# Four-layer cross attention: weight folds in two row groups of TensorE, three homes for their results, keys, values and wo requested elsewhere

## The chip, the cores and the metric

One core of a Trainium2 chip runs the whole program. The metric is the device time of one execution in microseconds, the median over runs.

## What is computed

`x` (4 x 1024 x 512) passes through four cross attentions on one context `ctx` (4 x 64 x 1024): grouped, masked, grouped, masked.

```
grouped: xn = rmsnorm(x) * norm_w; q = xn @ wq (16 heads of 32); k, v = ctx @ wk, ctx @ wv (4 heads of 32)
         x = x + softmax(q k^T / sqrt(32)) v @ wo
masked:  q = x @ Wq (16 heads of 64); k, v = ctx @ Wk, ctx @ Wv (16 heads of 64)
         logits = q k^T / 8 + bias of two pairs of key columns from the token masks
         x = x + softmax(logits) v @ Wo + bo
```

All is float32. TensorE multiplies most matrices in three products of a high part (rounded to the format fp32r) and the rest: hi*hi + hi*lo + lo*hi.

## The kernel before

**Folds.** In the masked layers Wq is multiplied into the keys and Wo into the values ahead of time: per layer, 8 key folds and 8 value folds, each for one pair of heads, 32 in all (`MASKED`). `m_made(n)` (24 matmuls of 256 columns) makes 128 rows (two heads of 64) of k^T or v^T for all four batches in bank `OB`. ScalarE (`kv_hi`) and VectorE (`kv_lo`) spread it as high and low part into `bd`, a 128 x 512 block diagonal tile, zero where a row's head isn't the column's. `folding(n)` multiplies it with the weight block `fhl`: 4 banks of 3 matmuls, each 512 columns wide over all 128 rows. `taken_out(n)` copies two banks by ScalarE and two by VectorE into a home in SBUF (`staged`, two homes in turn), and SyncE's queue stores them to DRAM in 4 transfers of 256 KB (`f_store`), beside the loads of 512 KB (`w_load`) and 256 KB (`f_load`) for each fold.

**Order.** It is written out by hand. PE runs `m_made(n)`, then `folding(n-1)`, for n = 0 to 23 (`EARLY`), with six small products for the grouped layers between (`g_made`); then the query product of the first token block (`q_bound`), and then `grouped_first`: 8 times scores of the grouped layer, `m_made`, `folding`. ScalarE's program for step n is `kv_hi(n)`, `w_hi(n+4)`, `taken_out(n-1)`, `f_hi(n+1)`; VectorE's `kv_lo(n)`, `w_lo(n+4)`, `taken_out(n-1)`, `f_lo(n+1)`. `folding(n)` waits until `taken_out(n-1)` has freed its banks. At n = 12 to 15 ScalarE also rounds the four pieces of the grouped layer's wq (`ws_hi`). At n = 20 it waits for `bias_b` twice counted, then rounds and squares two pieces of x (`x_hi`) into `xqhl` and `xsq`.

**GpSimd.** It scales wq by the norm weights (`ws_scale`), makes the bias of the second layer in the scratch tile `xsq`, waits for the four `ws_hi` with `ws_lo`, then makes the bias of the fourth layer in the same scratch, and counts `bias_b` (lines 1183 to 1226). That is why `x_hi`, which writes `xsq`, waits for it (line 748).

**After the folds** 8 rounds over batches and layer pairs (`body`) run on each of two token blocks; they load the folds back in 16 pieces of 256 KB through `ring`, the last 8 from `sFN` (`ring_load`, line 344). ScalarE rounds each and GpSimd takes the rest (`part_lo`, line 1260). The first round needs wo of the grouped layer in `wraw`, which SyncE requests after the last store (line 284).

Of the kernel before, what the change touches and what calls it, by code (L numbers as in the profile page):

```python
# [14 lines left out]
P = 128  # L15
BATCH = 4
# [26 lines left out]
def bass_cross_attention_stack(nc, xT, ctxT, wkvM, wkvG, wqG, woG, wqM, woM, normw, bo, masks, idx, xs):  # L43
# [12 lines left out]
    with ctx:  # L56
# [8 lines left out]
        sFN = nc.dram_tensor("s_fn", (PAIRS, BATCH, KC, P, D), F32, kind="Internal").ap()  # L65
        sKG = nc.dram_tensor("s_kg", (PAIRS, BATCH, 2, P, KEYS), F32, kind="Internal").ap()
# [47 lines left out]
        names = ("ctx_in cx_hi cx_lo w_hi w_lo made taken g_hi kv_hi f_hi f_lo folded ev_a ev_d "  # L114
# [8 lines left out]
        f_st = [sem(f"s_f_st{i}") for i in range(2)]  # L123
        wg_in = [sem(f"s_wg_in{i}") for i in range(2)]
# [14 lines left out]
        bd = [foldM[:, :, i, 0:HALF] for i in range(2)]  # L139
# [20 lines left out]
        def staged(n, o):  # L160

            if n % 2 == 0:
                return ring[:, o, :] if n < 8 else X[0][:, o, :]
            if n < EARLY:
                return prob[0][:, 2 + o // 2, (o % 2) * BLK:(o % 2 + 1) * BLK]
            return wraw[:, o, :]

        def pair(n, part, r):

            rows = slice(64 * r, 64 * r + 64)  # L170
            return bd[n % 2][rows, part, :].rearrange("p (b h k) -> p b h k", b=BATCH, h=2)[:, :, r, :]

        def t_bank(ph, t):

            return MX if ph in (0, 3) and t % 2 else TB

# [12 lines left out]
        def _(sp):  # L189
            sp.dma_start(cx, ctxT).then_inc(S["ctx_in"], 16)  # L190
            for n in range(2):
                sp.dma_start(wG[:, n], wkvG[0, n]).then_inc(wg_in[n], 16)
# [12 lines left out]
            def f_store(n):  # L205
                lp, t = n // (2 * KC), n % KC
                for o in range(4):
                    if o < 2:
                        sp.wait_ge(S["ev_a"], 2 * n + o + 1)
                    else:  # L210
                        sp.wait_ge(S["ev_d"], 2 * n + o - 1)
                    if n // KC % 2 == 0:
                        sp.dma_start(sFM[lp, t, o].rearrange("p b n -> p (b n)"), staged(n, o)).then_inc(f_st[n % 2], 16)
                    else:
                        sp.dma_start(sFN[lp, o, t], staged(n, o)).then_inc(f_st[n % 2], 16)

            def g_store(lp, i):
                sp.wait_ge(S["taken"], g_step(lp, i) + 1)
                if i == 0:
                    for b in range(BATCH):  # L220
                        sp.dma_start(sKG[lp, b].rearrange("s p k -> p s k"),
                                     stK[lp][:, :, b * KEYS:(b + 1) * KEYS].bitcast(F32)).then_inc(g_st[lp], 16)
                else:
                    sp.dma_start(sVG[lp, 2 * (i - 1):2 * i].rearrange("b k n -> (b k) n"),
                                 stV[lp][:, i - 1]).then_inc(g_st[lp], 16)

            def kg_load(it):
                for r in range(4):
                    sp.dma_start(kG4[32 * r:32 * r + 32, :, :, KEYS * r:KEYS * (r + 1)].bitcast(F32),
                                 sKG.rearrange("l b s (j d) k -> (l b) d s j k", d=HD_G)[it]).then_inc(S["ld_kg"], 16)  # L230
# [17 lines left out]
            for n in range(4, MASKED + 9):  # L248
                if n < MASKED:
                    w_load(n)  # L250
                if n == 5:
                    for i in range(GROUP):
                        g_store(0, i)
                    for i in range(2):
                        sp.dma_start(wG[:, i], wkvG[1, i]).then_inc(wg_in[i], 16)
# [4 lines left out]
                if n >= 9:  # L260
                    f_store(n - 9)
                if 4 <= n - 3 < MASKED:
# [3 lines left out]
                if n == 19:  # L266
                    sp.wait_ge(S["zero"], 3)
                    for i in range(PAIRS):
                        sp.wait_ge(g_st[i], (BATCH + 2) * 16)
                    kg_load(0)  # L270
                if n == 21:
                    vg_load(0)
                if n == 20:
                    sp.wait_ge(f_st[0], 4 * 64)
# [7 lines left out]
            sp.wait_ge(f_st[1], 16 * 64)  # L282
            sp.wait_ge(S["ws_lo"], DC)
            sp.dma_start(wraw[:, :, :], woG[0]).then_inc(S["ld_w"], 16)
            sp.wait_ge(f_st[0], 16 * 64)
            sp.dma_start(X[0][:, :, :], xT[0, 0]).then_inc(S["ld_x0"], 16)

            def body(it, lp, first, last):
# [43 lines left out]
                if not first:  # L332
# [10 lines left out]
                for t in range(KC):  # L343
                    ring_load(t % 4, sFN[lp, b, t], ("fb_lo", 12 * it + t + 1))
# [10 lines left out]
        def _(pe):  # L355
# [8 lines left out]
            pe.wait_ge(S["ctx_in"], 16)  # L364

            def g_made(lp, i):
# [3 lines left out]
                if i < 2:  # L370
                    pe.wait_ge(wg_in[i], 16 * (lp + 1))
                for c in range(CC):
                    if i == 0:
# [20 lines left out]
            def folding(n):  # L394
                if n == 0:
                    pe.wait_ge(S["zero"], 3)
                pe.wait_ge(S["taken"], m_step(n) + 1)
                pe.wait_ge(S["f_lo"], n + 1)
                w, kv = fhl[n % 2], bd[n % 2]
                for o in range(4):  # L400
                    cut = slice(o * P, (o + 1) * P)
                    if n > 0 and o < 2:
                        pe.wait_ge(S["ev_a"], 2 * n + o - 1)
                    elif n > 0:
                        pe.wait_ge(S["ev_d"], 2 * n + o - 3)
                    if n // KC % 2 == 0:
                        last = three(FB[o][:, :], w[:, 0, cut], w[:, 1, cut], kv[:, 0, :], kv[:, 1, :], True, True)
                    else:
# [972 lines left out]
```

## Time and profile before

| | us |
|---|---|
| median of 3 runs (1568.18 to 1569.41) | 1569.0 |
| the profiled execution | 1568.2 |
| its span, first to last instruction | 1566.4 |
| PE busy in it | 1549.7 |
| folds 0 to 23 and what makes them, on PE | 15.9 to 158.0 |
| folds 24 to 31, with grouped scores | 170.1 to 221.2 |

A timeline row gives start and length in us, engine, line, operation, written tile <- read tiles, and a count. Matmuls are pipelined, so lengths of neighbours overlap: the pace is the distance between starts. `three` (lines 359 to 361) issues nearly all matmuls, so rows are told apart by their tiles: `OB<-xhl,foldN` is `m_made` in the early part, `<-foldM,pT` and `<-pT,foldM` are folds.

### The profile page before, as it was taken

Reading aid. Unit: us, or ns where it says so; the run is one execution under the profiler, and the core shown is the slowest. Engines: PE = TensorE matmul, PEld = TensorE weight load, DVE = VectorE, ACT = ScalarE, POOL = GpSimd, SP = SyncE. Lnnn points to the kernel's source line nnn. Section 1 sums busy time; section 2 is a strip of 40 time slices with the busy share of each in tenths; the row PEclk is TensorE's granted clock in tenths of the full one; section 3 lists DMA queues with packets and bytes.
Section 4 is the critical chain, followed back from the end, with each engine's and each line's share of the span. In section 5 each row is a group of like instructions: output and inputs, shape, how many; then the busy total and the mean of one; then the engine's idle time right before and its main releaser. Section 6 shows DMA issues by size and latency. Waiting matters only on the chain.

```text
span 1566.4 us, 22435 instructions
## 1 busy us (share of the span) xinstructions
PE 1549.7 (99%) x8032; PEld 1260.3 (80%) x8032; DVE 1025.5 (65%) x1697; ACT 770.5 (49%) x1349; POOL 882.8 (56%) x809
## 2 busy tenths in 40 slices
PE   8999999999999999999999999999999999999998
PEld 7999887788778877788778877887778877887787
DVE  6777657765566657665776556665766577655664
ACT  4566666425643465335642564346533564256431
POOL 0523357546864676467754685467645775468431
PEclk9999999999999999999999999999999999999999
DMA  9999563122321331122312232133112231222101
GB/s 345 317 331 375 200 222 99 53 70 94 115 61 31 129 115 47 34 90 76 114 51 69 94 115 61 31 131 113 47 35 94 75 111 52 66 95 88 54 1 54
DMA packets 110237, 170.58 MB, mean 109 GB/s; under 512 B 27568, under 2 KB 60848, under 8 KB 103984
## 3 DMA queue, kind: packets, MB, share of 16 engines
q1 hardware_dynamic: 107232, 151.85, 29.7%
q10 hardware_dynamic: 2736, 16.78, 2.6%
q8 instruction: 65, 1.06, 0.3%
q0 software_dynamic: 160, 0.53, 0.1%
q14 instruction: 44, 0.36, 0.1%
HBM read 117.48 MB, written 51.65 MB: 108 GB/s over the span
## 4 chain that ended last, share of the span: by engine, by line
PE 94%; POOL 3%; DMA 1%; DVE 1%; ACT 0%; issue 0%; SPq 0%
PE OB L359 17%; PE OB L361 17%; PE OB L360 17%; PE SB L359 10%; PE SB L361 9%; PE SB L360 9%; PE TB L480 5%; PE MX L516 4%; PE MX L480 2%; POOL xhl L1268 1%; POOL prob L1233 1%; PE SB L459 1%; POOL prob L1239 1%; DMA prob<-in_wkvM_dram 1%; PE TB L361 0%; PE TB L359 0%
## 5 line engine op out<-in xcount | busy, mean ns | idle before, releaser
L1239 POOL TENSOR_TENSOR prob<-prob,small 128x512 f32<-128x512 f32 x256 | 277.8, 1088 | 288.7 <-DVE small L1041 288.7
L1233 POOL TENSOR_TENSOR prob<-prob,small 128x512 f32<-128x512 f32 x128 | 136.3, 1065 | 147.8 <-DVE small L1016 147.7
L1022 DVE SCALAR_TENSOR_TENSOR prob<-SB,aux 128x512 f32<-128x512 f32 x128 | 88.1, 688 | 198.9 <-PE SB L361 198.9
L359 PE MATMUL SB<-foldM,xhl 128*128 128x512 f32 x512 | 203.0, 396 | 4.5 <-POOL xhl L1268 2.7
L359 PE MATMUL OB<-pT,foldN 128*128 128x512 f32 x512 | 205.0, 400 | 0.0
L360 PE MATMUL OB<-pT,foldN 128*128 128x512 f32 x512 | 199.8, 390 | 0.0
L361 PE MATMUL OB<-pT,foldN 128*128 128x512 f32 x512 | 199.8, 390 | 0.0
L361 PE MATMUL SB<-foldM,xhl 128*128 128x512 f32 x512 | 199.6, 390 | 0.0
L360 PE MATMUL SB<-foldM,xhl 128*128 128x512 f32 x512 | 199.4, 389 | 0.0
L762 ACT ACTIVATE prob<-prob 128x512 f32<-128x512 f32 x128 | 80.5, 629 | 173.6 <-DVE prob L1028 172.2
L1016 DVE TENSOR_REDUCE small<-prob 128x8 f32<-128x512 f32 x128 | 87.4, 683 | 109.8 <-ACT prob L771 109.8
L480 PEld LDWEIGHTS TB<-ident,prob 128*128 128x128 f32 x768 | 90.3, 140 | 52.9 <-issue 32.5
L771 ACT ACTIVATE prob<-SB 128x512 f32<-128x512 f32 x128 | 76.5, 597 | 106.3 <-PE SB L361 102.6
L1247 POOL TENSOR_TENSOR xqhl<-ring,xqhl 128x512 fp32r<-128x512 f32 x64 | 82.9, 1306 | 69.4 <-ACT xqhl L702 69.4
L359 PEld LDWEIGHTS SB<-foldM,xhl 128*128 128x128 f32 x512 | 96.1, 188 | 31.9 <-POOL xhl L1268 9.8
L480 PE MATMUL TB<-ident,prob 128*128 128x128 f32 x768 | 117.7, 276 | 0.0
L1028 DVE TENSOR_TENSOR prob<-prob,small 128x512 f32<-128x512 f32 x128 | 111.1, 868 | 4.5
L361 PEld LDWEIGHTS OB<-pT,foldN 128*128 128x128 f32 x512 | 96.1, 188 | 20.9
L361 PEld LDWEIGHTS SB<-foldM,xhl 128*128 128x128 f32 x512 | 96.1, 188 | 20.7
L360 PEld LDWEIGHTS SB<-foldM,xhl 128*128 128x128 f32 x512 | 96.2, 188 | 19.2
L359 PEld LDWEIGHTS OB<-pT,foldN 128*128 128x128 f32 x512 | 96.4, 188 | 18.2 <-DVE pT L919 0.3
L360 PEld LDWEIGHTS OB<-pT,foldN 128*128 128x128 f32 x512 | 96.5, 188 | 17.1
(157 smaller groups left out, 3927.3 us busy)
## 6 DMA issues: line engine op xcount, KB each, us to landing
prob<-in_wkvM_dram SPq DMA_DIRECT2D x32, 512.0 KB, 6.4
ring<-s_fm SPq DMA_DIRECT2D x64, 256.0 KB, 5.1
ring<-s_fn SPq DMA_DIRECT2D x64, 256.0 KB, 2.7
out_dram<-x ACTq DMA_DIRECT2D x15, 1024.0 KB, 3.9
s_fm<-prob SPq DMA_DIRECT2D x32, 256.0 KB, 5.0
wraw<-in_wqG_dram SPq DMA_DIRECT2D x8, 1024.0 KB, 8.5
s_fn<-x SPq DMA_DIRECT2D x32, 256.0 KB, 4.9
ring<-in_xT_dram SPq DMA_DIRECT2D x32, 256.0 KB, 3.3
```

What stands on the lines that cost most here:

```text
L359: pe.matmul(out, a_hi, b_hi, start=start, stop=False)
L360: pe.matmul(out, a_hi, b_lo, start=False, stop=False)
L361: return pe.matmul(out, a_lo, b_hi, start=False, stop=stop)
L480: last = pe.transpose(out[:, tt * P:(tt + 1) * P], pr[:, tt, t * P:(t + 1) * P], ident[:, :])
L762: act.activation(own, own, ACT.Exp).then_inc(S["exped"], 1)
L771: act.activation(prob[ph][:, u % 4, (u // 4) * HALF:(u // 4 + 1) * HALF], SB[u % 2][:, :], ACT.Copy).then_inc(S["copied"], 1)
L1016: dve.reduce_max(hmax[u % 2], own, AX_X).then_inc(S["maxed"], 1)
L1022: dve.scalar_tensor_tensor(out=own, in0=bank, scalar=M_SCALE, in1=row, op0=ALU.mult, op1=ALU.add).then_inc(S["biased"], 1)
L1028: dve.tensor_tensor(own, own, hmax[u % 2].unsqueeze(2).broadcast_to([P, HH, KEYS]), ALU.subtract).then_inc(S["evac"], 1)
L1233: pool.tensor_tensor(own, own, hmax[u % 2].unsqueeze(2).broadcast_to([P, HH, KEYS]), ALU.subtract).then_inc(S["evac"], 1)
L1239: pool.tensor_tensor(own, own, rsum[u % 2].unsqueeze(2).broadcast_to([P, HH, KEYS]), ALU.mult).then_inc(S["normed"], 1)
L1247: pool.tensor_tensor(xqhl[:, 1, c % 2, :], ring[:, c, :], xqhl[:, 0, c % 2, :].bitcast(F32), ALU.subtract).then_inc(S["x_lo"], 1)
```

## The change

The folds work per head. `kv` holds the rows as they are (128 x 256, no zeros). Head 0 lies in rows 0 to 63 and head 1 in rows 64 to 127 of both operands; each matmul takes 64 rows, and the two heads' alternate and write different banks. A key fold has 24 matmuls of 64 rows x 256 columns, a value fold 12 of 64 rows x 512 columns. ScalarE takes out head 0's banks, VectorE head 1's. There are six homes and stores of 512 KB; folds 8 to 23 use three in turn. `sFN` and `sKG` have other layouts: a piece of `sFN` comes back in two transfers of 64 partitions, and the grouped keys are stored in one transfer with rows of 1 KB. The first loads are split in halves. ScalarE requests the first grouped keys at its steps 12 to 15; the grouped values and wo are requested by SyncE after the store of fold 29. wq goes to `wraw` later (SyncE's n = 16 where it was 11), and ScalarE rounds it at its steps 17 to 20, where it was 12 to 15. VectorE's first four memsets are gone. GpSimd's program is as it was.

```diff
-        bd = [foldM[:, :, i, 0:HALF] for i in range(2)]
+        kv = [foldM[:, :, i, 0:BATCH * KEYS] for i in range(2)]
...
+        STAGES = (ring, lower, upper, X[0], wraw, X[1])
+        HOME = ((0, 2, 4, 0, 2, 4, 0, 2) + (3, 1, 2) * 5 + (3,)
+                + (4, 3, 4, 3, 4, 3, 5, 3))
...
@@ sync @@
+                    sp.dma_start(dst, staged(n)[:, 2 * i:2 * i + 2, :]).then_inc(f_st[HOME[n]], 16)
...
+                if n - 9 == MASKED - 3:
+                    sp.wait_ge(f_st[4], 32 * stores(4))
+                    sp.wait_ge(S["ws_lo"], DC)
+                    sp.dma_start(wraw[:, :, :], woG[0]).then_inc(S["ld_w"], 16)
...
+                    vg_load(0)
...
-                if n == 11:
+                if n == 16:
+                    sp.wait_ge(f_st[4], 32 * 2)
                     sp.dma_start(wraw[:, :, :], wqG[0]).then_inc(S["ld_w"], 16)
...
                 for t in range(KC):
-                    ring_load(t % 4, sFN[lp, b, t], ("fb_lo", 12 * it + t + 1))
+                    sp.wait_ge(S["fb_lo"], 12 * it + t + 1)
+                    for r in range(2):
+                        sp.dma_start(ring[64 * r:64 * r + 64, t % 4, :],
+                                     sFN[lp, t, b // 2, r, 64 * (b % 2):64 * (b % 2) + 64, :]).then_inc(ld_ring[t % 4], 16)
@@ tensor, folding(n) @@
+                w, x = fhl[n % 2], kv[n % 2]
+                parts = ((0, 0), (0, 1), (1, 0))
+                for i in range(2):
+                    if n > 0:
+                        pe.wait_ge(S["ev_a"], 2 * n + i - 1)
+                        pe.wait_ge(S["ev_d"], 2 * n + i - 1)
+                    for a in range(2 if n // KC % 2 == 0 else 1):
+                        for m, (p, q) in enumerate(parts):
+                            for r in range(2):
+                                rows = slice(64 * r, 64 * r + 64)
+                                if n // KC % 2 == 0:
+                                    cut = slice((2 * i + a) * P, (2 * i + a + 1) * P)
+                                    last = pe.matmul(FB[2 * i + r][:, 256 * a:256 * a + 256], w[rows, p, cut], x[rows, q, :],
+                                                     start=(m == 0), stop=(m == 2))
+                                else:
+                                    last = pe.matmul(FB[2 * i + r][:, :], x[rows, p, i * P:(i + 1) * P], w[rows, q, :],
+                                                     start=(m == 0), stop=(m == 2))
                     last.then_inc(S["folded"], 1)
@@ scalar @@
-                for r in range(2):
-                    src = OB[m_step(n) % 2][64 * r:64 * r + 64, 0:BATCH * KEYS].rearrange("p (b k) -> p b k", b=BATCH)
-                    last = act.activation(pair(n, 0, r), src, ACT.Copy)
+                act.activation(kv[n % 2][:, 0, :], OB[m_step(n) % 2][:, 0:BATCH * KEYS], ACT.Copy).then_inc(S["kv_hi"], 1)
...
-                if 12 <= n < 12 + DC:
-                    ws_hi(0, n - 12)
+                if 17 <= n < 17 + DC:
+                    ws_hi(0, n - 17)
+                if 12 <= n < 16:
...
+                    act.dma_start(*kg_part(0, n - 12)).then_inc(S["ld_kg"], 16)
                 if n == 20:
                     for i in range(PAIRS):
-                        act.wait_ge(g_st[i], (BATCH + 2) * 16)
+                        act.wait_ge(g_st[i], 3 * 16)
                     act.wait_ge(S["bias_b"], PAIRS)
                     x_hi(0, 0, 0, True)
                     x_hi(0, 0, 1, True)
@@ vector, kv_lo(n): one operation of 128 x 256 for two of 64 x 256; taken_out as ScalarE's @@
```

## Rows read from the trace of the kernel before

**Rows 1.** The page, part 1: span and PE's busy time, share, count.
```profile
span 1566.4 us, 22435 instructions
PE 1549.7 (99%) x8032; PEld 1260.3 (80%) x8032; DVE 1025.5 (65%) x1697; ACT 770.5 (49%) x1349; POOL 882.8 (56%) x809
```
**Rows 2.** Windows: stretch, length, busy us by engine (count), granted clock, DMA share, GB/s.
```profile
100.00:120.00 20.00, 20.00 (x131) 18.31 (x130) 16.68 (x22) 12.79 (x24) 10.53 (x17) 1.00 1.01 334
120.00:140.00 20.00, 20.00 (x131) 18.25 (x130) 15.48 (x23) 12.72 (x23) 6.93 (x11) 1.00 1.04 401
...
178.00:197.00 19.00, 19.00 (x128) 17.52 (x127) 17.70 (x30) 13.80 (x25) 6.91 (x7) 1.00 0.75 263
```
**Rows 3.** PE's timeline: two folds' first matmuls, one make's, two folds' among scores.
```profile
21.75 0.40 PE L359 MATMUL OB<-foldM,pT 128*128 128x512 f32 x1
...
24.50 0.28 PE L359 MATMUL OB<-xhl,foldN 128*128 128x256 f32 x1
...
27.37 0.40 PE L359 MATMUL OB<-foldM,pT 128*128 128x512 f32 x1
...
177.65 0.40 PE L359 MATMUL OB<-pT,foldM 128*128 128x512 f32 x1
...
183.99 0.40 PE L359 MATMUL OB<-pT,foldM 128*128 128x512 f32 x1
```
**Rows 4.** PE's timeline: eight loads with one-column matmuls, then column tiles of 64.
```profile
169.25 0.95 PE L459 MATMUL SB<-small,sqsum 128*128 128x1 f32 x8
170.06 0.37 PE L359 MATMUL SB<-kG,foldM 128*128 128x256 f32 x1
...
239.55 0.39 PE L361 MATMUL OB<-foldN,wqo 128*128 128x512 f32 x1
239.87 1.08 PE L516 MATMUL MX<-pF,vG 128*64 128x512 f32 x4
240.88 0.33 PE L480 MATMUL TB<-ident,prob 128*128 128x128 f32 x1
```
**Rows 5.** The weight loads' timeline (PEld) at those column tiles.
```profile
239.87 0.20 PEld L516 LDWEIGHTS MX<-pF,vG 128*64 128x64 f32 x4 [0.36 <-issue]
```
**Rows 6.** ScalarE's timeline in its step n = 20.
```profile
135.76 0.77 ACT L685 ACTIVATE foldM<-OB 64x256 fp32r<-64x256 f32 x2 [0.38 <-PE OB L361]
136.55 1.06 ACT L669 ACTIVATE foldN<-prob 128x1024 fp32r<-128x1024 f32 x1
...
139.67 0.63 ACT L702 ACTIVATE xqhl<-ring 128x512 fp32r<-128x512 f32 x1
```
**Rows 7.** Groups by form, 60 to 150 us: busy us, mean ns, idle before.
```profile
L919 DVE TENSOR_TENSOR foldN<-prob,foldN 128x1024 fp32r<-128x1024 f32 x17 | 21.9, 1288 | 3.7 <-ACT foldN L669 3.6
...
L919 DVE TENSOR_TENSOR foldM<-OB,foldM 64x256 fp32r<-64x256 f32 x32 | 13.5, 422 | 11.7 <-ACT foldM L685 11.5
...
L962 DVE COPY prob<-TB 128x512 f32<-128x512 f32 x8 | 5.5, 692 | 1.1 <-DMA s_fn<-prob 0.8
```
**Rows 8.** GpSimd's timeline: the last ws_lo, and the store after the second bias.
```profile
111.90 1.29 POOL L1165 TENSOR_TENSOR wqo<-wraw,wqo 128x512 fp32r<-128x512 f32 x1 [4.49 <-ACT wqo L719]
...
127.11 0.61 POOL L1226 DMA_DIRECT2D s_aux<-aux  x1 [0.31 <-POOL aux L1224]
```
**Rows 9.** PE's timeline: the same 16 matmuls after idling and in midstream.
```profile
7.04 5.24 PE L374 MATMUL OB<-prob,x 128*128 128x256 f32 x16 [7.04 <-DMA x<-in_wkvG_dram]
...
35.74 3.61 PE L374 MATMUL OB<-prob,x 128*128 128x256 f32 x16
```
**Rows 10.** SyncE's timeline: the requests for the grouped keys.
```profile
92.71 1.94 SPq L229 DMA_DIRECT2D kG<-s_kg  x4
```
**Rows 11.** PE's timeline after wo has come.
```profile
231.37 1.08 PE L516 MATMUL MX<-pF,vG 128*64 128x512 f32 x4 [0.93 <-ACT pF L779]
```
**Rows 12.** GpSimd's timeline: the first round's first piece of sFN split.
```profile
278.31 1.28 POOL L1262 TENSOR_TENSOR foldN<-ring,foldN 128x512 fp32r<-128x512 f32 x1
```
**Rows 13.** PE's timeline: the product that reads that piece.
```profile
302.97 0.47 PE L359 MATMUL OB<-pT,foldN 128*128 128x512 f32 x1
```

More of the change, by code:

```diff
@@ L112, in bass_cross_attention_stack @@
         FB = [OB[2], OB[3], TB, MX]
-        names = ("ctx_in cx_hi cx_lo w_hi w_lo made taken g_hi kv_hi f_hi f_lo folded ev_a ev_d "
+        names = ("cx_hi cx_lo w_hi w_lo made taken g_hi kv_hi f_hi f_lo folded ev_a ev_d "
                  "ld_w ws_scaled ws_hi ws_lo c_in c_norm "
@@ L254, in _ @@
                     for i in range(2):
-                        sp.dma_start(wG[:, i], wkvG[1, i]).then_inc(wg_in[i], 16)
+                        for h in range(2):
+                            sp.dma_start(wG[:, i, 4 * h:4 * h + 4], wkvG[1, i, :, 4 * h:4 * h + 4]).then_inc(wg_in[2 * i + h], 16)
                     f_load(2)
@@ L331, in body @@
                 sp.dma_start(aux[:, :], sAux[lp]).then_inc(S["ld_aux"], 16)
-                if not first:
+                if first:
+                    sp.wait_ge(f_st[5], 32 * stores(5))
+                else:
                     sp.wait_ge(S["stored1"], 16 * it)
@@ L361, in three @@
                 return pe.matmul(out, a_lo, b_hi, start=False, stop=stop)
[L364 removed]
+            pe.wait_ge(cx_in[0], 16)
             def g_made(lp, i):
@@ L511, in mixing @@
                     pe.wait_ge(S["ld_vg"], 64 * (it + 1))
+                    if first and ph == 1:
+                        pe.wait_ge(S["ev_d"], 2 * MASKED)
                 if j > 0 or ph == 2:
@@ L785, in part_hi @@
             def part_hi(it, i, first):
-                act.wait_ge(ld_ring[i % 4], 16 * (6 * it + (2 if i < 4 and not first else 3 + i // 4)))
+                if i < 4:
+                    act.wait_ge(ld_ring[i % 4], 16 * (8 * it + (3 if first else 2)))
+                else:
+                    act.wait_ge(ld_ring[i % 4], 16 * (8 * it + 2 * (1 + i // 4)))
                 act.activation(fold_part(i, 0), ring[:, i % 4, :], ACT.Copy).then_inc(S["fold_hi"], 1)
@@ L923, in _ @@
             dve.memset(small[:, 12:16], -0.5).then_inc(S["idented"], 1)
-            for i in range(2):
-                for part in range(2):
-                    last = dve.memset(bd[i][:, part, :].bitcast(F32), 0.0)
-            last.then_inc(S["zero"], 1)
             dve.memset(kG[:, :, :].bitcast(F32), 0.0).then_inc(S["zero"], 1)
@@ L949, in kv_lo @@
                 dve.wait_ge(S["kv_hi"], n + 1)
-                for r in range(2):
-                    src = OB[m_step(n) % 2][64 * r:64 * r + 64, 0:BATCH * KEYS].rearrange("p (b k) -> p b k", b=BATCH)
-                    last = lo_part(pair(n, 1, r), src, pair(n, 0, r))
-                last.then_inc(S["taken"], 1)
+                lo_part(kv[n % 2][:, 1, :], OB[m_step(n) % 2][:, 0:BATCH * KEYS], kv[n % 2][:, 0, :]).then_inc(S["taken"], 1)
             def taken_out(n):
-                for o in range(2, 4):
-                    dve.wait_ge(S["folded"], 4 * n + o + 1)
-                    if n >= 2 and o == 2:
-                        dve.wait_ge(f_st[n % 2], 64 * (n // 2))
-                    if n == EARLY + 1 and o == 2:
+                for i in range(2):
+                    dve.wait_ge(S["folded"], 2 * n + i + 1)
+                    if uses(n) and i == 0:
+                        dve.wait_ge(f_st[HOME[n]], 32 * uses(n))
+                    if n == EARLY and i == 0:
                         dve.wait_ge(S["ws_lo"], DC)
-                    dve.tensor_copy(staged(n, o), FB[o][:, :]).then_inc(S["ev_d"], 1)
+                    to, out = own(n, i, 1)
+                    dve.tensor_copy(to, out).then_inc(S["ev_d"], 1)
             for h in range(2):
```

137 lines of the change are left out of this document (65 added, 72 removed).

## The prediction

> **What bounds the kernel now.** The page comes first: PE is busy for 1549.7 of 1566.4 us [rows 1], so whatever shortens the run has to take time off PE or fill one of its few gaps. The windows over the fold stretch come next: the granted clock is 1.00, PE is full, and at the same time the DMA engines' share is 1.01 to 1.04 [rows 2]. Two things are near their limit there, PE and memory traffic, and the reader is to see that traffic was 334 GB/s in one window and 401 in the next, with PE's matmul count alike. PE's timeline then prices a step: a fold runs from 21.75 to 24.50, 2.75 us for 12 matmuls of 512 columns (0.229 each); the make up to 27.37 takes 2.87 for 24 of 256 (0.120 each). A step is 5.62. Among the scores it is 183.99 - 177.65 = 6.34 [rows 3]. The rest of the run, 8 rounds at full PE, is touched by the change only through smaller transfers.
>
> **The fold on PE.** The same products are done without the zeros. If both row groups stream at once, a key fold is 12 pairs of 256 columns, 12 x 0.120 = 1.44 us, a value fold 6 pairs of 512, 6 x 0.229 = 1.37. No row shows row groups. The nearest are the column groups of `mixing`: four passes of 512 columns, started at 239.87, are over at 240.88 [rows 4]. One after another they would take at least four times 0.427 (the pace of 512 columns in two passes; two of 0.213 by the 0.229 less its overhead), 1.7 us, so the two groups do overlap; and their four weight loads lie within 0.20 us [rows 5]. I take full overlap. The bounds are 1.37 and, without overlap, 24 x 0.120 = 2.87.
>
> Between full and tiled use PE pays. The matmul before `mixing` starts at 239.55 and has streamed by 239.78; the tiled one starts at 239.87, 0.09 later. On both ways the first weight load, elsewhere hidden, lies bare: eight loads with a one-column matmul each take 170.06 - 169.25 = 0.81, about 0.10 each [rows 4]. So 0.4 us per fold, bounds 0.2 and 0.5. A key fold comes to 1.84 (saves 0.91), a value fold to 1.77 (saves 0.98). Folds 0 to 23 are 16 and 8 of them: 14.6 + 7.8 = 22.4 us. PE's step is then 4.71.
>
> One rule speaks against this. The Trainium skill, "TensorE: Matmul & The Clock Gate", section on LDWEIGHTS, has a load priced by its columns and not by its rows, so that a load of 64 rows costs as much as one of 128. Its page "TensorEngine Tiling (Array Packing)", key properties, lets different tiles load in parallel, and says that a change of mode drains the engine. The 0.10 of the one-column row agrees with the first, the 0.20 us for four loads with the second, the 0.09 with the third. If the loads of two row groups came one after another, a key fold would gain nothing: that is rival C.
>
> **The other engines in a step.** ScalarE's step is 0.4 for keys (one operation for two of 0.38), 1.06, two copies of 0.5, 0.5 for the weights: 3.1 us, 3.7 with `ws_hi` [rows 6]. Each request for grouped keys is 1.94 / 4 = 0.49 [rows 10]; on ScalarE it makes steps 12 to 15 3.6 us, or 4.1 if one takes twice as long: still under 4.71, so nothing. VectorE loses one of two 0.42 operations and keeps 1.29, two of 0.69 and the weights' part, under 4 us [rows 7]. Copies with strided targets are like the strided 64 x 256 ones of now, at no more per element.
>
> **DMA.** A step moves 512 + 256 + 4 x 256 KB = 1.835 MB. In 4.71 us that is 390 GB/s; one window shows 401, another 334 at a share of 1.01 [rows 2]. I take 401 as possible, since it was had when SyncE had requests in arrears, and charge 2 us for folds 0 to 19 (0 to 12.5: at 334 a step is 5.49 and 16 steps give up 0.78 each). Three homes take away waits of the copies for a store; none of those reached PE before, so 0 by itself. The Trainium skill, "DMA: Bandwidth & Descriptors", specifications, gives a core about 358 GB/s of HBM; by it a step would be at least 5.1 us. The row of 401 contradicts it here.
>
> **The new wait.** This is the term that I weigh most. `x_hi` at ScalarE's n = 20 waits for the second bias, because it writes the scratch in which GpSimd makes it. GpSimd starts that bias only after the last `ws_lo`, and so after the last `ws_hi`. From the start of that `ws_lo`, 111.90, to the count just before the store, 127.11 - 0.31 = 126.80, it takes 14.9 us [rows 8]. Before, ScalarE came to `x_hi` at 139.67 [rows 6], 12.9 us after that. Now the last `ws_hi` is itself at n = 20, directly ahead of the wait. GpSimd's program is unchanged, so ScalarE stands for 14.9 us. What is queued behind: `x_hi` and squares (four starts 0.52 apart, 2.1), `kv_hi(21)`, `w_hi(25)`, `taken_out(20)`. From the end of `m_made(20)`: `ws_hi` ends at 3.8, the bias at 18.7, x at 20.8, `kv_hi(21)` at 21.2, `w_hi(25)` at 22.2; VectorE's `w_lo(25)` ends at 23.5, its first copy of fold 20 at 24.2, and `folding(21)` can start at 24.3. PE meanwhile has done two folds and two makes, 2 x 4.71 = 9.4. It idles 14.9 us (bounds 12.5, if GpSimd runs faster beside idle neighbours, and 15.5). Then it starts slow: the same 16 matmuls took 5.24 us after 7.04 us of idling and 3.61 in midstream, 1.6 more [rows 9] (0 to 3). After that every wait for `taken_out` is met again.
>
> **Folds among scores.** 8 value folds save 0.98 on PE, step 5.36. VectorE was busy 17.70 of 19 us, 5.9 per step, in the first ones [rows 2]; less 0.42 that is 5.5, and it becomes the bound for four of them: 4 x 0.84 + 4 x 0.98 = 7.3 us (5 to 7.9).
>
> **wo and grouped values.** wo lands two steps earlier. PE's gap of 0.93 behind it [rows 11] goes: 0.9 (0 to 0.9). wq later: SyncE asks for it with the store of fold 7, some nine steps (42 us) before ScalarE's step 17, and scaling takes GpSimd a few operations like those in rows 8: nothing.
>
> **Halved transfers of sFN.** 64 more requests on SyncE, which is idle most of a round. The first piece is ready on GpSimd at 278.31 + 1.28 = 279.6 and is multiplied at 302.97 [rows 12, 13]: 23 us of cover; 0, and if it were gone 0.5 us per piece.
>
> **First loads, memsets.** Making starts when the second masked weight block has landed behind all earlier bytes, and these are the same: 0 (-1 to +1).
>
> **Sum.** -22.4 + 14.9 + 1.6 + 2.0 - 7.3 - 0.9 = -12.1. The profiled execution took 1568.2, which gives 1556.1; the median of before is 0.8 above it, so **1557 us**.
>
> **Rivals.**
> A. The second bias is not waited for at length (it ends earlier than I read, or something frees ScalarE). Then 16.5 fall away: 1568.2 - 28.6 + 0.8 = 1540. For it: GpSimd is idle most of this stretch. Against it: the order of GpSimd's program, fixed.
> B. Memory traffic bounds folds 4 to 19 at the 334 GB/s of the weaker window: 12.5 for the 2.0, less what the stand lets it catch up, sum -1.6: 1567. For it: share above 1 at 334. Against it: 401.
> C. The weight loads of the two row groups come one after another. A key fold is 24 x 0.101 + 0.4 = 2.82 (+0.07), value folds keep their gain (12 loads in 1.21). 16 x 0.07 - 7.8, PE idles 24.3 - 11.4 = 12.9, + 1.6 - 7.3 - 0.9 = -0.4: 1569. For it: 0.10 per load. Against it: four loads in 0.20.
> D, on the other side: row groups do not overlap at all. Key folds 24 x 0.120 + 0.4 = 3.28 (+0.53), value folds 12 x 0.229 + 0.4 = 3.15 (+0.40); 11.7 in the first 24, 12.0 + 1.6 for the wait, 3.2 among scores, -0.9: +27.6, **1597**. It turns from gain to loss once a pair takes over about 0.19 us in place of 0.12. For it: no row has row groups, and none has tiles in fp32r. Against it: `mixing`.
>
> **How the numbers follow.** Forecast 0.60 (its own range 1550 to 1564, from the bounds of the terms), A 0.07, B 0.14, C 0.08, D 0.11. What can't be told from no change is 0.2%, 3 us. Faster: the forecast, A and most of B (0.09), 0.76; within: the rest of B and C, 0.13; slower: D, 0.11. The range 1541 to 1572 leaves out D and half of A.
>
> **What would show it.** Row pairs started a few ns apart and 1.4 us of streaming per fold (against C, D); a step of 4.7 on PE before fold 20; one gap of about 15 us on PE near 125 us with ScalarE waiting for GpSimd's aux, and slow matmuls behind it; then steps of 5.4 to 5.5 among the scores; no gap before the first `mixing`; rounds 2 to 8 as long as before. I am wrong if that gap is absent, if a pair takes the time of two, or if steps before it are over 5 us with SyncE never waiting.

## The result, and the profile after

The changed kernel takes **1558.7 us** (median of 4 runs, 1558.5 to 1560.3), the kernel before 1569.2 beside it (1568.2 to 1569.6). The ratio is 0.9938 [0.9924, 0.9951]; the forecast was 1557. The profiled execution took 1558.5 us with a span of 1556.7; before they were 1568.2 and 1566.4 [rows 1], so the spans differ by 9.7. The first `mixing` starts 9.70 earlier than before (221.67 for 231.37) and one of the last round 9.60 (1471.42 for 1481.02): all of it lies ahead of 240 us, and rounds 2 to 8 are as long as before.

The fold on TensorE (PE in the rows), the first key fold behind the last of the grouped products (start and length in us, engine, line, operation, written tile <- read tiles, count). It answers to [rows 3].

```profile
54.62 0.98 PE L431 MATMUL OB<-foldM,pT 64*128 64x256 f32 x12
55.91 0.28 PE L431 MATMUL TB<-foldM,pT 64*128 64x256 f32 x1
55.92 0.28 PE L431 MATMUL MX<-foldM,pT 64*128 64x256 f32 x1
56.03 0.28 PE L431 MATMUL TB<-foldM,pT 64*128 64x256 f32 x1
56.04 0.28 PE L431 MATMUL MX<-foldM,pT 64*128 64x256 f32 x1
56.24 0.39 PE L379 MATMUL OB<-xhl,foldN 128*128 128x256 f32 x1
```

Two matmuls of different row groups start 10 ns apart, a pair each 0.12 us, and the fold is over after 56.24 - 54.62 = 1.62 us, where it took 2.75. The make behind it is longer, 3.06 for 2.87. A value fold takes 1.59 and its step 4.64.

Then the long gap. First TensorE, then ScalarE, GpSimd and VectorE of the changed kernel around it; the bracket is the idle time before the row and who ended it:

```profile
129.79 0.28 PE L381 MATMUL OB<-xhl,foldN 128*128 128x256 f32 x1
144.87 1.65 PE L431 MATMUL OB<-foldM,pT 64*128 64x256 f32 x12 [14.80 <-DVE x L993]
147.72 0.58 PE L379 MATMUL OB<-xhl,foldN 128*128 128x256 f32 x1
155.59 0.97 PE L431 MATMUL OB<-foldM,pT 64*128 64x256 f32 x12 [1.75 <-DVE prob L993]
```

```profile
124.42 0.60 ACT L723 ACTIVATE prob<-OB 128x512 f32<-128x512 f32 x1 [1.29 <-DMA s_fm<-prob]
125.91 0.63 ACT L747 ACTIVATE wqo<-wraw 128x512 fp32r<-128x512 f32 x1
138.54 0.63 ACT L730 ACTIVATE xqhl<-ring 128x512 fp32r<-128x512 f32 x1 [11.99 <-POOL aux L1255]
140.63 0.36 ACT L711 ACTIVATE foldM<-OB 128x256 fp32r<-128x256 f32 x1
140.89 1.04 ACT L699 ACTIVATE foldN<-prob 128x1024 fp32r<-128x1024 f32 x1
```

```profile
126.62 1.28 POOL L1196 TENSOR_TENSOR wqo<-wraw,wqo 128x512 fp32r<-128x512 f32 x1 [3.33 <-ACT wqo L747]
127.89 3.33 POOL L1223 TENSOR_SCALAR xsq<-xsq,sqsum 128x64 f32<-128x64 f32 x8
137.11 1.26 POOL L1255 TENSOR_TENSOR aux<-aux,spare 128x512 f32<-128x512 f32 x1
```

```profile
141.02 0.42 DVE L956 TENSOR_TENSOR foldM<-OB,foldM 128x256 fp32r<-128x256 f32 x1 [14.28 <-ACT foldM L711]
141.97 2.15 DVE L956 TENSOR_TENSOR foldN<-prob,foldN 128x1024 fp32r<-128x1024 f32 x1 [0.52 <-ACT foldN L699]
144.04 0.68 DVE L993 COPY x<-OB 128x512 f32<-128x512 f32 x1
```

Read from the back: fold 21 waits for VectorE's copy, VectorE stood 14.28 us for ScalarE's `kv_hi`, ScalarE stood 11.99 us in front of `x_hi` for GpSimd's `aux`, and GpSimd began that bias only after the last `ws_lo`. PE's row says "<-DVE", but the cause is three engines back. The 1.75 before fold 23 (the last PE row) is another matter, taken up with the first experiment.

The windows of the changed kernel (busy time of each engine, then granted clock, DMA share, GB/s), against [rows 2]:

```profile
60.00:80.00 20.00, 20.00 (x178) 17.60 (x175) 14.62 (x22) 12.65 (x23) 0.80 (x1) 1.00 1.02 391
80.00:100.00 20.00, 20.00 (x159) 17.33 (x158) 17.18 (x23) 12.17 (x22) 19.18 (x30) 1.00 1.05 405
100.00:120.00 20.00, 19.77 (x191) 18.26 (x189) 13.93 (x20) 11.16 (x20) 4.14 (x4) 1.00 1.05 402
134.00:144.00 10.00, 0.00 (x0) 0.00 (x0) 2.46 (x2) 5.46 (x11) 8.38 (x10) 0.50 0.25 96
144.00:158.00 14.00, 11.39 (x99) 10.63 (x100) 10.07 (x16) 6.38 (x11) 0.00 (x0) 0.76 0.93 296
```

DMA kept 391 to 405 GB/s for 60 us. TensorE's granted clock fell to 0.50, the lower of its two levels, within the gap and stayed there until 150.8: fold 21 took 2.85 us and the make behind it 4.42.

Two folds among the scores of the changed kernel, 5.36 us apart where it was 6.34:

```profile
176.69 0.96 PE L434 MATMUL OB<-pT,foldM 64*128 64x512 f32 x6
182.05 0.73 PE L434 MATMUL OB<-pT,foldM 64*128 64x512 f32 x4
```

**Where the time went**, by the same landmarks in both traces (after less before, running total): first make 17.66 for 15.92, +1.7. Fold 20 starts at 125.32 for 141.18, -15.9, so the twenty steps from fold 0 to fold 19, with the makes beside them, brought 17.6. Query product at 157.20 for 158.08, -0.9: the stretch with the gap costs 15.0 net. Second query product at 212.29 for 221.15, -8.9: scores brought 8.0, of which the eight folds 7.8. The gap of 0.93 before the first `mixing` [rows 11] is gone, -9.7, the difference of the spans.

### The profile page after: what moved, and what is told of

The parts are those of the page before. It is cut to its first block, busy times and chain, and to the rows that moved or that the text cites. A ratio compares the mean times of both kernels' runs of the same rounds, so it can differ in the third digit from the quotient of the medians.

```text
span 1556.7 us, 22870 instructions
## 1 busy us (share of the span) xinstructions
PE 1522.4 (98%) x8224; PEld 1233.7 (79%) x8224; DVE 1004.1 (64%) x1661; ACT 750.1 (48%) x1317; POOL 881.2 (57%) x809
## 4 chain that ended last, share of the span: by engine, by line
PE 90%; POOL 4%; DVE 2%; DMA 1%; ACT 1%; issue 1%; SPq 1%; ACTq 0%; DVEq 0%; POOLq 0%
PE OB L379 16%; PE OB L381 15%; PE OB L380 15%; PE SB L379 10%; PE SB L381 9%; PE SB L380 9%; PE TB L508 5%; PE MX L546 4%; POOL xhl L1299 2%; PE MX L508 2%; POOL prob L1264 1%; PE SB L487 1%; DMA s_fm<-prob 1%; PE OB L434 1%; PE OB L431 1%
```

## Experiments

All are variants of the changed kernel but one; each was timed against the kernel before. Kernels that have undivided first loads count lines from `three` on three to five lower, that with wo last one lower.

### Where the long gap comes from

**Weights rounded early.** ScalarE rounds wq at its steps 12 to 15 again.

```diff
-                if 17 <= n < 17 + DC:
-                    ws_hi(0, n - 17)
+                if 12 <= n < 12 + DC:
+                    ws_hi(0, n - 12)
```

> The changed kernel, with ScalarE rounding wq at its steps 12 to 15 as before and not 17 to 20; all else as changed. My theory: the 14.8 us for which PE idles at 130 us, the slow clock after it (2.6 us over the fold at 144.87 and the make at 147.72) and the 1.75 us gap before fold 23 all come from x_hi waiting for the second bias. GpSimd will have done its first bias at 100.8, four ws_lo by 106 and the second bias by about 119, before ScalarE comes to x_hi at 126. Then 19 us go, less 1 to 3 us for folds 20 to 23, which memory traffic (400 to 410 GB/s from 70 to 134 us) will hold up: 1541 to 1543 us, no gap over 3 us before 160 us. Rival 1 (the stand only shows a backlog of DMA that has to be drained anyway, landings being 10 us and more late): PE idles 8 to 12 us somewhere before 158 us, 1552 us or more. Rival 2 (the stand is x_hi's wait for its pieces of x or for the grouped stores): nothing changes, 1558.

Measured 1544.95 us, 0.9848 [0.9835, 0.9862]. The gap of 14.8 is gone and `x_hi` does not wait. But 13.7 us came back and not the whole of gap and slow clock, and the time is 2 us above what was expected. There is a new, small gap; VectorE and GpSimd of this kernel at that place, and TensorE with every gap of 0.3 us and more from there to the query product:

```profile
102.74 5.40 DVE L956 TENSOR_TENSOR foldN<-prob,foldN 128x1024 fp32r<-128x1024 f32 x1 [0.53 <-ACT foldN L699]
108.07 0.68 DVE L993 COPY prob<-OB 128x512 f32<-128x512 f32 x1
```

```profile
102.01 5.02 POOL L1196 TENSOR_TENSOR wqo<-wraw,wqo 128x512 fp32r<-128x512 f32 x4
107.02 5.70 POOL L1223 TENSOR_SCALAR xsq<-xsq,sqsum 128x64 f32<-128x64 f32 x8
```

```profile
108.89 0.86 PE L431 MATMUL OB<-foldM,pT 64*128 64x256 f32 x10 [2.92 <-DVE prob L993]
141.89 0.98 PE L431 MATMUL OB<-foldM,pT 64*128 64x256 f32 x12 [1.75 <-DVE prob L993]
```

VectorE's `w_lo`, elsewhere 1.23 us, takes 5.40 and ends at 108.14: 1.1 us after 107.03, when GpSimd's four `ws_lo` in a row were over. PE idles 2.92 and then runs 3.4 us at 0.5.

The second row shows that the 1.75 before fold 23 has nothing to do with the long gap: it stands here too. Folds 22 and 23 follow each other with no make between, so fold 23 waits for VectorE's copies of fold 22, and VectorE is held up by `kv_lo` and `w_lo` before them. From the start of fold 22 to that of fold 23 it is 3.44 us here, with folds of 1.62 and a gap of 1.75, and again 3.44 with folds of 1.96 (heads in turn, gap 1.40) and of 3.06 (one row group, gap 0.31). In the kernel before, with folds of 2.75, fold 23 follows after 2.82 without a gap. It is the faster fold that lays this wait bare.

**Bias first.** GpSimd makes the second bias ahead of the four `ws_lo`; the weights stay late.

```diff
-                    for c in range(DC):
-                        ws_lo(0, c)
...
+            for c in range(DC):
+                ws_lo(0, c)
```

> The changed kernel with one move on GpSimd alone: the second bias is made ahead of the four ws_lo. ScalarE's program is as changed. My theory: the bias is then done at about 114 us, x_hi waits for nothing, and the time is that of the experiment that rounds wq early, within 1 us: 1541 to 1543. Rival 1 (DMA backlog): 1552 or more. Rival 2 (it was rounding wq at steps 17 to 20 that made ScalarE late, not the wait): 1555 to 1558.

1546.92 us, 0.9861 [0.9848, 0.9875]. The order on GpSimd alone removes the long gap too. It is 4 us above what was expected: gaps of 1.41 and 2.00 stand in its place, beside the 1.75 before fold 23; at the first, `f_lo` took 3.38 us beside two `ws_lo` in a row.

**The late weights in the kernel before.** wq requested at SyncE's step 16 and rounded at 17 to 20, all else as before.

```diff
-                if n == 11:
+                if n == 16:
                     sp.dma_start(wraw[:, :, :], wqG[0]).then_inc(S["ld_w"], 16)
...
-                if 12 <= n < 12 + DC:
-                    ws_hi(0, n - 12)
+                if 17 <= n < 17 + DC:
+                    ws_hi(0, n - 17)
```

> The kernel before with one part of the change alone: wq requested at SyncE's n = 16 and rounded at ScalarE's steps 17 to 20. My theory: the stand comes from this move alone, whatever the folds cost. From the end of the make of step 20: wq rounded at 4.2, bias 12.2 later (as measured after the change) at 16.4, x at 18.5, keys, weights and VectorE's copy until fold 21 can start at 22.4; PE is busy for two of its steps, 11.2, so it idles 11 us, and then runs slow for 2 to 3 us: 1569.2 + 13 to 14 = 1583. Rival (the stand needs the faster folds, the longer steps of before give GpSimd the time): 1569 to 1571.

1582.35 us, 1.0086 [1.0069, 1.0102], 13.9 more than the kernel before beside it (1568.46), as expected. PE idles 10.34 before fold 21. The same row appears on its ScalarE, with nothing else of the change present:

```profile
152.75 0.63 ACT L702 ACTIVATE xqhl<-ring 128x512 fp32r<-128x512 f32 x1 [12.50 <-POOL aux L1224]
```

So the late weights cost 13.9 in the old kernel and 13.7 in the new one, and the rest of the change gives about 24.

### What the row groups give

**One row group.** Both heads read rows 0 to 63, in the same matmul count and shapes; the products of head 1's rows are left out.

```diff
-                                rows = slice(64 * r, 64 * r + 64)
+                                rows = slice(0, 64)
```

> The changed kernel with both heads' fold matmuls reading rows 0 to 63 of both operands; head 1's rows are left out of the folds. Instructions, banks, waits and order are the same, but neighbours are in one row group and cannot overlap. My theory: row groups alone give the gain. A key fold then takes 24 x 0.120 + 0.15 = 3.0 and a value fold 12 x 0.229 + 0.15 = 2.9 instead of 1.6 each; 32 x 1.35 = 43, less 3 at the idle time before fold 21: +40, 1599 us. Rival (a matmul of 64 rows streams faster by itself): folds of 1.6 to 2.2 us and under 1575. The trial with the heads in turn, which cost 3.3 us only, is explained by my theory only if TensorE drew the other group's matmuls ahead; here it can't, so a fold must show 2.9 to 3.1.

1597.72 us, 1.0187 [1.0173, 1.0201], as expected. TensorE of this kernel at a fold's end:

```profile
26.30 0.28 PE L431 MATMUL TB<-foldM,pT 64*128 64x256 f32 x1
26.42 0.28 PE L431 MATMUL MX<-foldM,pT 64*128 64x256 f32 x1
26.54 0.28 PE L431 MATMUL TB<-foldM,pT 64*128 64x256 f32 x1
26.66 0.28 PE L431 MATMUL MX<-foldM,pT 64*128 64x256 f32 x1
26.87 0.38 PE L379 MATMUL OB<-xhl,foldN 128*128 128x256 f32 x1
```

The same rows follow each other at 0.12 where they fell in pairs. Key folds take 3.06, value folds 2.94. That the two groups overlap is worth 39 us, and without it the change would lose: rival D's mechanism, at about its price.

**Heads in turn.** The loop over heads goes outside, so that a bank pair is done for head 0 and then for head 1.

```diff
-                    for a in range(2 if n // KC % 2 == 0 else 1):
-                        for m, (p, q) in enumerate(parts):
-                            for r in range(2):
+                    for r in range(2):
+                        for a in range(2 if n // KC % 2 == 0 else 1):
+                            for m, (p, q) in enumerate(parts):
```

> The changed kernel with the two heads' matmuls of a fold no longer alternating: all of head 0's of a half fold, then all of head 1's. Same instructions, other order. My theory: the gain of the folds is the overlap of neighbouring matmuls in different row groups. Without it a key fold takes 24 x 0.120 and a value fold 12 x 0.229 plus the change of mode, about 1.5 us more each; the idle time before fold 21 shrinks by 3 us, since PE is busy longer beside it. 32 x 1.5 - 3 - 1 = +44: 1602 us. Rival 1 (memory traffic bounds the early steps anyway, PE has room): only the 8 folds among scores lose, +12: 1571. Rival 2 (TensorE finds the overlap by itself, pulling the other group's matmuls ahead): 1559.

1561.99 us, 0.9959 [0.9944, 0.9974]: missed by 40. TensorE of this kernel, in the same key fold:

```profile
62.56 0.28 PE L431 MATMUL OB<-foldM,pT 64*128 64x256 f32 x1
62.56 0.28 PE L431 MATMUL TB<-foldM,pT 64*128 64x256 f32 x1
62.92 0.28 PE L431 MATMUL MX<-foldM,pT 64*128 64x256 f32 x1
62.92 0.28 PE L431 MATMUL TB<-foldM,pT 64*128 64x256 f32 x1
63.15 0.52 PE L431 MATMUL MX<-foldM,pT 64*128 64x256 f32 x3
```

In each pair above one matmul stands three instructions behind the other in the program; the first of TB started at 62.45, ahead of the last two of OB (62.56 and 62.68), which come before it. Matmuls of a free row group are started ahead of those of a busy one. Only the ends of a fold stay alone, and a key fold takes 1.96 for 1.62, a value fold 1.59 as before. Alternating in the code is worth 3.3 us, not 40.

### The parts priced at nothing

**Two homes.** Folds 8 to 23 use two homes in turn.

```diff
-        HOME = ((0, 2, 4, 0, 2, 4, 0, 2) + (3, 1, 2) * 5 + (3,)
+        HOME = ((0, 2, 4, 0, 2, 4, 0, 2) + (1, 3) * 8
```

> The changed kernel with folds 8 to 23 in two homes in turn (lower, X[0]) instead of three. Stores land 7 to 13 us after their request between 100 and 130 us, with steps of 4.64 us. My theory: two homes give a store 9.3 us less the copies, so copies wait and PE with them from about fold 12 on: PE loses 0.5 to 2 us a step until SyncE and DMA are in step, 3 to 10 us before the stand at 130 us, none after it: 1562 to 1569. Rival (DMA throughput, not homes, sets the pace; the third home only moves the wait from the copies to the loads): 1558 to 1560, within 0.1%.

1564.03 us, 0.997 [0.9959, 0.9982], 5.4 more than the change, in the range expected. ScalarE of this kernel:

```profile
102.65 0.60 ACT L723 ACTIVATE prob<-OB 128x512 f32<-128x512 f32 x1 [3.42 <-DMA s_fn<-prob]
109.15 0.60 ACT L723 ACTIVATE x<-OB 128x512 f32<-128x512 f32 x1 [3.68 <-DMA s_fn<-x]
```

The copies wait for the store of the fold before last, and PE idles 1.06, 1.33 and 1.80 behind them, with 3.4 us at 0.5 after the last.

**Whole first loads.** Context and weight blocks each come in one transfer again.

```diff
-            for h in range(2):
-                sp.dma_start(cx[:, 4 * h:4 * h + 4], ctxT[:, 4 * h:4 * h + 4]).then_inc(cx_in[h], 16)
-                sp.dma_start(wG[:, 0, 4 * h:4 * h + 4], wkvG[0, 0, :, 4 * h:4 * h + 4]).then_inc(wg_in[h], 16)
-            for h in range(2):
-                sp.dma_start(wG[:, 1, 4 * h:4 * h + 4], wkvG[0, 1, :, 4 * h:4 * h + 4]).then_inc(wg_in[2 + h], 16)
+            sp.dma_start(cx, ctxT).then_inc(cx_in[0], 16)
+            for i in range(2):
+                sp.dma_start(wG[:, i], wkvG[0, i]).then_inc(wg_in[2 * i], 16)
```

> The changed kernel with the first loads whole as before (context 1 MB, each grouped weight 512 KB) instead of in halves. My theory: the halves, with rows of 2 and 4 KB, moved 258 GB/s in the stretch 2 to 6 us where whole ones moved 355, so the second masked weight block landed at 13.1 and not at 11.4, and the first make began at 17.66 and not at 15.92. With whole loads the first make starts at 15.9 to 16.1 and the time falls by 1.7 us to 1557. Rival (the three additional requests on SyncE, 0.45 us each, are what is late, not the bytes): the same 1.3 to 1.7 us, but with DMA at 336 or more in both kernels' stretch 2 to 6 us. Rival 2 (it is the product order or VectorE's missing memsets): first make still at 17.6, 1558.6.

1557.12 us (1556.9 to 1557.3), 0.9924 [0.9911, 0.9938], 1.5 less than the change. The stretch from 4 to 6 us of its windows, and of the changed kernel's:

```profile
4.00:6.00 2.00, 0.00 (x0) 0.00 (x0) 0.15 (x1) 0.43 (x1) 0.00 (x0) 1.00 0.97 399
```

```profile
4.00:6.00 2.00, 0.00 (x0) 0.00 (x0) 0.19 (x2) 1.06 (x1) 0.00 (x0) 1.00 0.96 266
```

The share of busy DMA time is the same, but half loads move 266 GB/s where whole ones move 399. That holds in every trace of this document: 256 to 296 GB/s in these 2 us in the seven kernels with halves, 375 to 401 in the seven with whole loads. Halves are both smaller and in rows half as long, and no run separates the two. The first make starts at 16.92 for 17.66, and not at 15.92 as before. In this kernel the clock rose at 12.9 us, in the kernel before at 10.2; over the other kernels it lay between 9.6 and 13.1, so part of a start is chance. Over all traces the first make starts at 17.47 to 18.66 with halves and at 15.92 to 17.03 with whole loads, so the halves can account for all of the 1.7.

**wo and grouped values last.** Both requests move behind the last store.

```diff
-                if n - 9 == MASKED - 3:
-                    sp.wait_ge(f_st[4], 32 * stores(4))
-                    sp.wait_ge(S["ws_lo"], DC)
-                    sp.dma_start(wraw[:, :, :], woG[0]).then_inc(S["ld_w"], 16)
...
-                    vg_load(0)
```

> The changed kernel with wo and the grouped values requested after the last fold's store, as wo was before. My theory: PE's gap of 0.8 to 0.9 us at the first mixing comes back, and the four requests for the values in front of the token block add up to 2 us to what mixing waits for: 1559.5 to 1561.5. Rival (nothing on the path, since the second query product covers it): 1558.6.

1563.2 us, 0.9961 [0.9948, 0.9975], 4.5 more than the change and 2 more than expected at most. The profiled execution is the longest of the five, 1565.7. SyncE's queue, ScalarE and the first `mixing` of this kernel:

```profile
215.85 1.19 SPq L295 DMA_DIRECT2D wraw<-in_woG_dram  x1
217.13 3.78 SPq L252 DMA_DIRECT2D vG<-s_vg  x4
221.76 6.17 SPq L322 DMA_DIRECT2D ring<-s_fm  x4
```

```profile
225.05 0.63 ACT L746 ACTIVATE wqo<-wraw 128x512 fp32r<-128x512 f32 x1 [6.02 <-DMA wraw<-in_woG_dram]
227.25 1.23 PE L545 MATMUL MX<-pF,vG 128*64 128x512 f32 x4 [3.56 <-ACT pF L811]
```

What `mixing` waits for is wo: ScalarE stands 6.02 us until it has landed, 8 us after its request was through, and only then comes to the `pF` that `mixing` reads. In the kernel before ScalarE stood 3.39 at that place. The values' four requests come behind that of wo, so they can't delay the request; why wo takes longer to land than in the kernel before (4.7 us) is open. PE idles 3.56 and runs 3.4 us at 0.5. This trace also has a late first make (18.29 for 17.66) and 3.4 us of slow clock behind the gap before fold 23, so not all of the 4.5 need be wo's.

### A better version

**Early weights and whole first loads** (the first and the fourth edit together).

> The changed kernel with wq rounded at steps 12 to 15 and with whole first loads together. If the two gains are apart: 1558.7 - 17 - 1.7 = 1540. If memory traffic is the bound for folds 4 to 23 once the stand is gone, the 1.7 us of the start are kept, since bytes come sooner too; if PE then only waits longer for DMA, 1541.5, as with the first alone.

1543.73 us (1543.3 to 1545.6), 0.9841 [0.9827, 0.9854]. That is 2 us and more above both figures expected. The gap beside the four `ws_lo` remains, 2.40, and so does the 1.75 before fold 23.

**Weights spaced.** The same with `ws_hi` at steps 14 to 17, so that `ws_lo` don't run four in a row.

```diff
-                if 17 <= n < 17 + DC:
-                    ws_hi(0, n - 17)
+                if 14 <= n < 14 + DC:
+                    ws_hi(0, n - 14)
```

> The kernel with whole first loads and early rounding of wq (1543.7), with wq rounded at ScalarE's steps 14 to 17 instead of 12 to 15. In that one GpSimd was late with the first bias and then ran its four ws_lo in a row from 102.0 to 107.0; VectorE's w_lo, which began at 102.7, took 5.40 us instead of 1.2 to 1.3, PE idled 2.4 us and ran 3.4 us at the granted clock 0.5. My theory: VectorE's operation was held up by GpSimd's row of operations without a break. With the roundings later than the first bias, each ws_lo runs alone, no w_lo takes over 2.6 us there, the gap and the slow clock go: 3 to 4 us less, 1540. Second bias done at about 122, x_hi wanted at 125. Rival (the long w_lo comes from traffic into SBUF, 400 GB/s then, not from GpSimd): still one w_lo over 4 us and 1543 to 1544. Rival 2 (once PE is not held up, it meets the DMA backlog two folds later): 1542 to 1543.

1545.26 us, 0.9849 [0.9835, 0.9862], a miss. `w_lo` took 3.09 beside two `ws_lo`, and that gap shrank to 0.60. But the second bias was done at 125.65 only, `x_hi` waited 1.26 us, its own four operations take 2.1, and PE idled 3.46 at 128.74 and was slow for 6.8.

**Spaced, and x one step later** (the block of `n == 20` at 21).

```diff
-                if n == 20:
+                if n == 21:
```

> The kernel of e8 (whole first loads, weights rounded at n = 14 to 17) with ScalarE's block of x_hi moved from n = 20 to n = 21. There x_hi waited 1.26 us for a bias that was done at 125.65, and TensorE idled 3.46 us and then ran at half clock for 6.8 us. My theory: one step (4.6 us) later the bias is done before ScalarE comes, the gap of 3.46 and its slow stretch go (3.46 + about half of the folds' work in 6.8, less what VectorE makes up: 4 to 5 us), the 0.60 gap near 104 stays: 1545.3 - 4 to 5 = 1540 to 1541.5. Rival: the gap was VectorE's, stretched beside GpSimd's run of bias operations, and only moves: 1544 to 1546.

1543.65 us (1542.9 to 1544.8), 0.9841 [0.9827, 0.9854]: below the last, 2 us above what I expected. Nothing waits for the bias. PE idles 0.88, 0.27, 1.83 and 1.32 (the last before fold 23), and runs 6.8 us slow. VectorE, GpSimd and ScalarE of this kernel, and its window:

```profile
132.44 2.23 DVE L951 TENSOR_TENSOR foldN<-prob,foldN 128x1024 fp32r<-128x1024 f32 x1 [0.53 <-ACT foldN L694]
```

```profile
132.29 1.29 POOL L1281 TENSOR_TENSOR sqsum<-xsq 128x512 f32<-128x512 f32 x1
```

```profile
113.55 0.60 ACT L718 ACTIVATE x<-OB 128x512 f32<-128x512 f32 x1 [3.26 <-DMA s_fn<-x]
118.57 0.60 ACT L718 ACTIVATE prob<-OB 128x512 f32<-128x512 f32 x1 [2.20 <-DMA s_fn<-prob]
```

```profile
120.00:140.00 20.00, 16.85 (x176) 15.72 (x174) 16.35 (x21) 13.54 (x25) 9.15 (x8) 0.92 1.05 409
```

Two causes are left. `w_lo` is again late beside GpSimd, now the sum of squares behind `x_lo`; it ends at 134.67, 1.1 us after that. And with no long gap in which stores could catch up, copies wait for stores while DMA moves 399 to 409 GB/s at a share of 1.05: memory traffic is next.

**Late weights, x late** (whole first loads, `ws_hi` at 17 to 20, the x block at 23).

```diff
-                if n == 20:
+                if n == 23:
```

> The changed kernel with whole first loads, and ScalarE's block that waits for the second bias and rounds x_hi moved from n = 20 to n = 23; the weights are still rounded at n = 17 to 20, so that GpSimd rounds one low part at a time. My theory: the 14.8 us that TensorE idles comes from ScalarE standing in front of x_hi (bias ready at 138.4 to 138.7) with fold 21's evictions queued behind it. With the block three steps later ScalarE arrives at it near 139 to 143 and stands under 1 us, VectorE's operations are stretched only by single operations of GpSimd (under 2 us each), and TensorE keeps full clock: first folds to scores without a gap over 1 us, total 1557.1 - 15.7 + 0 to 1 = 1541 to 1542. Rival (x is the path): x_hi, x_lo and their store leave so late that the query product waits 2 us or more in front of its transfer, and the slow clock comes back: 1544 to 1548. Rival (GpSimd's bias stretches VectorE as much as the low parts did): a gap of 1 to 3 us among folds 19 to 23, 1545 to 1547.

1546.78 us, 0.986 [0.9847, 0.9873], 5 us above the theory. The first rival holds: ScalarE waited only 3.44 us, and with no fold behind it, but `x_lo` was then the last thing before the query product, which stood 4.80 us for it. The gap before fold 23 is 2.13, with VectorE's copy waiting 0.28 for a store.

The best are two at 1543.7 us, 25 us below the kernel before and 15 below the change, and which of them is the faster can't be told.

## Why the prediction was right

**The fold on PE** was -22.4. A fold takes 1.6, not 1.8, but the next make takes 0.19 more; the forecast had put a bare weight load on both sides of the fold. A step saves 0.94 (keys) or 0.98 (values), where 0.91 and 0.98 stood. Twelve and eight of them are 19.1 before fold 20. The Trainium skill, "TensorEngine Tiling (Array Packing)", key properties, says that tiles load and multiply in parallel; the pairs 10 ns apart agree. The order of the two heads in the program is worth little: 3.3 us, by heads in turn.

**DMA** was +2.0 up to fold 20. The trace has 19.1 less 17.6 = 1.5, of which gaps on PE are 1.18: 0.51 at 41.67, behind a step of the grouped products, and 0.23 and 0.44 at fold 18 and 19, where copies had waited 0.6 us for a store. Traffic like the 401 was indeed possible. Rival B was wrong for this kernel; once the long gap goes it comes back as waits of copies for stores. The 358 GB/s that the Trainium skill, "DMA: Bandwidth & Descriptors", specifications, gives a core does not hold here; further on the same page measures up to 425 with the neighbour core idle, and the Trainium skill, "Perfetto Trace Analysis", section on the roofline, names 435 as the ceiling of a lone core. The 409 agrees with these.

**The new wait** was 14.9 and is 14.80, with the chain of engines as forecast. The agreement in size is partly luck, because terms that were each off by 1 to 3 us cancel. Counted from the end of `m_made(20)` at 120.64, the last `ws_hi` ended after 5.9 us and not 3.8: ScalarE's copies had waited 1.89 and 1.29 us for stores, a wait that the forecast had at nothing. GpSimd then needed 11.8 us from the start of the last `ws_lo` to the count, not 14.9. Its eight operations on L1223 took 3.33 us while VectorE stood idle; they took 4.76 in the kernel before and 5.70 with the weights early, both beside a busy VectorE, and 3.34 in the old kernel with late weights, where VectorE stood too. My lower bound of 12.5 for the gap named that case. Behind `x_hi`, `w_lo` took 2.15 for 1.2, beside GpSimd's sum of squares. So fold 21 started 24.2 us after `m_made(20)`, for 24.3. The wait's share of the result is shown twice over, by early weights (-13.7) and by late weights alone in the old kernel (+13.9).

**The gap before fold 23**, 1.75, was not in the sum at all. The forecast took every fold to have a make behind it in which the copies are covered; fold 22 has none.

**Slow start** was +1.6 and is 1.2 for fold 21 and 1.4 for the make behind it, 2.6.

**Rival A** had 1540 without the long wait. The first try gave 1545. The wait was read rightly; wrong was that nothing would come in its place. `w_lo` is held up by the four `ws_lo` in a row (2.92 and a slow stretch), and the first loads (+1.7) and the gap before fold 23 (1.75) are in this kernel as well.

**Folds among scores** were -7.3 with VectorE as the bound in four of them. All steps are 5.36, -7.8: PE stayed the bound.

**First loads** were 0 and are +1.7, of which whole loads take back 0.7 at the first make and 1.5 of the total. The bytes were indeed the same; what I did not price is that the halves move at a lower rate in the first microseconds.

**Three homes** were 0 and are worth 5.4. The argument was that no wait for a store reached PE before. That held for a step of 5.62. At 4.64 the same stores are late. A cover has to be measured against the new step, not the old one.

**wo and values** were -0.9 for wo alone, and the gap went. Early requests of both are worth up to 4.5: asked for last, wo is what the first `mixing` waits for. What the values add to that isn't shown, since both moved together.

In sum by the trace: 1.7 - 17.6 + 15.0 - 8.0 - 0.8 = -9.7, for the -12.1 forecast. The same stretches in the forecast are 0, -16.8 (18.8 for twenty folds, less 2.0), +12.9 (the wait and slow start less four folds), -7.3 and -0.9. So the first loads are 1.7 over and the stretch with the gap 2.1, of which the gap before fold 23 is 1.75; the steps before it and the scores gave 1.5 back. That is 2.4 of the spans; the medians, 1558.7 for 1557, show 1.7.

## What to carry to other kernels

When a change makes the bounding engine faster, go again through every wait that was free at the old pace: stores, homes and rounding steps got late here without being touched. When work is moved on one engine, follow what the other engines' fixed order hangs on it; a wait directly behind it, for a scratch tile, took 14 us. And spread GpSimd's large tensor-tensor operations: a VectorE operation that reads two tiles in SBUF and starts among them is held until the last is over.

## What was not expected of the hardware

- VectorE's operation with two operands in SBUF was not served between GpSimd's 128x512 tensor-tensor operations but after the last of a run: `w_lo` took 5.40 us beside four and 3.09 beside two, for 1.23 alone, and `f_lo` 3.38 beside two, for 0.69. In four traces `w_lo` ended 1.1 us after GpSimd's last (108.14 for 107.03, 104.23 for 103.14, 134.67 for 133.58, 144.12 for 143.03), whatever its start. Who starts first doesn't settle which of the two is held: with weights early a `w_lo` from 116.52 took its 1.24, and GpSimd's operation at 116.83 took 1.84 for 1.04; but the `f_lo` of 3.38, with bias first, had started at 117.41, ahead of the first `ws_lo` at 117.67. The Trainium skill, "SBUF — State Buffer", section on who interferes with whom, has the two share a port pair that is held for a whole instruction, where GpSimd too reads SBUF. The traces agree that the two hold each other up, and add that back-to-back instructions leave no opening.
- TensorE starts matmuls of a free row group ahead of earlier ones of a busy group (62.45 ahead of 62.56 and 62.68).
- A gap of one length did or did not cost clock. The 1.75 before fold 23 was followed by 3.4 us at the lower level with bias first, whole first loads, two homes and wo last, and by none in the changed kernel, with early weights, with both together and with weights spaced. Gaps of 1.80, 2.40 and 2.92 were each followed by 3.4 us of it, one of 2.00 was not; the gap of 14.80 had 17.1 us at the lower level in and behind it.
- Half loads moved 266 GB/s and whole ones 399 in the same 2 us, at a DMA share of 0.96 and 0.97.
